# Two graph layers on one core: first tiles from contiguous copies, identity matmuls meanwhile, split products in another order, variances by Square, a ring of six tiles in layer 1, last y's steps moved by two tiles

## The reference

```
a1 = adj @ x;  a2 = adj @ x2                      # both times (2 + eps), then three dense layers each
h  = relu(h @ W[l].T + b[l])   for l in 0, 1, 2   # 128 x 128, one set of weights per branch
x  = layernorm(x + concat(h1, h2) @ Wm.T + bm)
A  = adj + I;  d = rsqrt(row sums of A)           # 0 where the sum is not positive
x  = layernorm(x + (d * (A @ (d * x))) @ W.T + b)
```

## Time and profile before

| | |
|---|---|
| median of 3 runs | 609.15 us (608.16 to 609.58) |
| the profiled execution | 609.65 us, its span 607.9 us |
| PE, matmuls | 589.8 us, 97% |
| DVE | 546.0 us, 90% |
| ACT | 368.5 us, 61% |
| DMA, mean | 233 GB/s |
| chain that ended last | PE 87%, DVE 9%, DMA, ACT and issue 1% each |

### The profile page before, as it was taken

One profiled execution on the slowest core, in us unless ns is written; L12 is line 12 of the kernel. 1 busy time (PEld: TensorE's weight loads), 2 busy tenths in 40 slices (PEclk: granted clock), 3 DMA queues, 4 the chain that ended last, 5 costly groups with the idle time before them and its releaser, 6 DMA issues.

```text
span 607.9 us, 7948 instructions
## 1 busy us (share of the span) xinstructions
PE 589.8 (97%) x2660; PEld 481.2 (79%) x2660; DVE 546.0 (90%) x697; ACT 368.5 (61%) x446; POOL 27.6 (5%) x31
## 2 busy tenths in 40 slices
PE   4999999999999999999999999999989999999996
PEld 3888888888888888888888888867758778778885
DVE  5999988997988997998799999966898988998997
ACT  6454337753454773363676355585867787787783
POOL 1000000001100000110000110000200010010011
PEclk9999999999999999999999999999999999999998
DMA  8968555433554533455543376584779999899921
GB/s 294 414 238 284 201 209 202 144 139 139 202 187 176 197 138 138 140 205 207 182 163 138 150 282 242 210 332 167 272 292 344 342 386 392 341 309 392 385 103 37
DMA packets 27833, 141.56 MB, mean 233 GB/s; under 512 B 2592, under 2 KB 3360, under 8 KB 13600
## 3 DMA queue, kind: packets, MB, share of 16 engines
q1 hardware_dynamic: 27376, 139.67, 62.2%
q10 hardware_dynamic: 432, 1.57, 0.6%
HBM read 139.14 MB, written 2.10 MB: 232 GB/s over the span
## 4 chain that ended last, share of the span: by engine, by line
PE 87%; DVE 9%; issue 1%; DMA 1%; ACT 1%; POOLq 0%; POOL 0%; SPq 0%; DVEq 0%; ACTq 0%
PE ps L409 75%; DVE alo L733 6%; PE pd L427 6%; PE ps L485 3%; PE pd L438 2%; PE pd L471 1%; DMA raw<-a_t 1%; DVE stats L805 1%; DVE z L906 1%; ACT ahi L582 1%; DVE mv L813 0%; DVE x1lo L872 0%; DVE xn L874 0%; DVE raw L888 0%; DVE raw L895 0%
## 5 line engine op out<-in xcount | busy, mean ns | idle before, releaser
L582 ACT ACTIVATE ahi<-raw 128x1024 fp32r<-128x1024 f32 x253 | 265.5, 1059 | 209.6 <-PE ps L409 196.6
L733 DVE TENSOR_TENSOR alo<-raw,ahi 128x1024 fp32r<-128x1024 f32 x253 | 304.7, 1217 | 46.6 <-ACT ahi L582 45.6
L409 PE MATMUL ps<-ahi,x2s 128*128 128x512 f32 x512 | 160.0, 391 | 0.0
L409 PE MATMUL ps<-ahi,x1hi 128*128 128x512 f32 x448 | 145.3, 400 | 12.0 <-DVE alo L726 8.0
L409 PE MATMUL ps<-alo,x1hi 128*128 128x512 f32 x448 | 141.2, 391 | 0.0
L409 PE MATMUL ps<-ahi,x1lo 128*128 128x512 f32 x448 | 141.0, 391 | 0.0
L409 PEld LDWEIGHTS ps<-ahi,x2s 128*128 128x128 f32 x512 | 96.7, 189 | 20.2
L409 PEld LDWEIGHTS ps<-ahi,x1hi 128*128 128x128 f32 x448 | 82.4, 189 | 37.3 <-issue 13.3
L409 PEld LDWEIGHTS ps<-alo,x1hi 128*128 128x128 f32 x448 | 84.6, 189 | 17.8
L409 PEld LDWEIGHTS ps<-ahi,x1lo 128*128 128x128 f32 x448 | 84.4, 188 | 17.8
L409 PE MATMUL ps<-alo,x2s 128*128 128x512 f32 x256 | 80.7, 391 | 0.0
(11 more groups left out here) (80 smaller groups left out, 348.7 us busy)
## 6 DMA issues: line engine op xcount, KB each, us to landing
raw<-a_t SPq DMA_DIRECT2D x108, 1024.0 KB, 4.8
raw<-a_t SPq DMA_DIRECT2D x39, 512.0 KB, 7.4
xn<-x SPq DMA_DIRECT2D x3, 1024.0 KB, 8.2
out<-outn ACTq DMA_DIRECT2D x3, 512.0 KB, 4.1
par<-params SPq DMA_DIRECT2D x1, 708.0 KB, 13.8
xn<-x SPq DMA_DIRECT2D x2, 256.0 KB, 4.8
raw<-a_t SPq DMA_DIRECT2D x2, 256.0 KB, 5.0
xn<-x SPq DMA_DIRECT2D x1, 512.0 KB, 7.9
```

The lines of the kernel that those rows point to most:

```text
L409: mm = pe.matmul(ps[bank][:, :], block_of(w, n), a[c], start=(n == 0 and k == 0), stop=(n == JB - 1 and k == 2))
L582: act.activation(ring_hi(n, last), raw_tile(layer, n), ACT.Copy).then_inc(hi_ready, 1)
L733: dve.tensor_tensor(ring_lo(n, last), raw_tile(layer, n), as_f32(ring_hi(n, last)), ALU.subtract).then_inc(lo_ready, 1)
```

## The change

- Start: three DRAM arrays take the place of strided reads: `head` (two halves of tile 0), `early` (tiles 1 to 7) and x12 in pieces. The first x piece is issued by ACT, not SP, so the halves of tile 0 are the first on SP. ACT rounds x's half of the piece, half a tile, x2's half, the other half.
- PE multiplies the identity by itself 8 times (128 x 128, float32) before tile 0; POOL makes the identity first.
- In every tile but those of the last quarter, PE takes the products with `ahi` first (hi by hi, hi by lo), then those with `alo`, and waits for `alo` only there.
- Layer 1: the ring has six places; the new ones are `hhi` and `alo_extra`. ACT and DVE steps beside layer 1 move by two tiles (`AHEAD_OF_PE`), among them `evacuate` from 2 to 4 and `copy_ay` from 1 to 3.
- The residual base of quarter 3 (two DVE instructions) moves from layer 1's tiles 7 and 8 to layer 0's tiles 20 and 21; the last y's bias from tile 24 to 30; its normalisation goes in blocks of four at tiles 20 and 21.
- Layer 1's variances: `accum_out` of residual2 gives the sum of z, ACT's Square with `accum_out` the sum of squares; bn_stats and bn_aggr go (but for the last quarter's tail).
- PE's loop over layer 1's quarters 1 and 2 is written out, since six does not divide 32.

```diff
-ACT_EVACUATE = 2
-ACT_RELU = tuple({k + SPLIT: l for k, l in plan.items()} for plan in PE_DENSE)
-DVE_RESIDUAL = tuple(k + SPLIT for k in PE_MERGE)
+PE_WARM = 8
+AHEAD_OF_PE = (SPLIT, SPLIT2)
+ACT_EVACUATE = (2, 4)
+ACT_RELU = tuple({k + ahead: l for k, l in plan.items()} for plan, ahead in zip(PE_DENSE, AHEAD_OF_PE))
+DVE_RESIDUAL = tuple(k + ahead for k, ahead in zip(PE_MERGE, AHEAD_OF_PE))
...
+        def slot(layer, q, n):
+            return (q * JB + n) % SPLIT2 if layer == 1 else n % SPLIT
...
+        def used_ahead(layer, q, n):
+            at = q * JB + (layer * QUARTERS * JB + n + 1)
+            if layer == 1 and q * JB + n >= SPLIT:
+                return at - SPLIT2 if q * JB + n >= SPLIT2 else 0
+            return at - SPLIT
...
-            load_x(0)
             for c in range(CH):
-                cols = slice(c * CW, (c + 1) * CW)
-                sp.dma_start(raw[:, 0, 0, cols], a_t[0][:, 0, cols]).then_inc(half_in[c], 16)
-            sp.dma_start(raw[:, 0, 1], a_t[0][:, 1]).then_inc(raw_in[0], 16)
+                sp.dma_start(raw[:, 0, 0, c * CW:(c + 1) * CW], head[c]).then_inc(half_in[c], 16)
+            sp.dma_start(raw[:, 0, 1], early[0]).then_inc(raw_in[0], 16)
...
+                    order = [(b, c, k) for b, c in banks for k in (0, 2, 1)]
+                else:
+                    order = [(b, c, k) for b in range(len(stationary)) for k in (0, 2) for c in range(CH)]
+                    order += [(b, c, 1) for b in range(len(stationary)) for c in range(CH)]
...
+                    if k == 1 and not lo_seen and not first:
+                        wait(pe, lo_ready, at)
+                        lo_seen = True
...
+            pe.wait_ge(warm_ready, 1)
+            for k in range(PE_WARM):
+                pe.matmul(pd[:, 3, 0:P], identity[:, :], identity[:, :], start=True, stop=True)
             layer0_quarter(0, None)
...
-                if n == ACT_EVACUATE:
+                if n == ACT_EVACUATE[plan]:
                     evacuate(q)
...
+            def square(q, blocks):
+                if blocks[0] == 0:
+                    wait(act, nmean_ready, q + 1)
+                    wait(act, out_written, q * 16)
+                for k in blocks:
+                    act.activation(outn[:, k * P:(k + 1) * P], z[:, k, :], ACT.Square, bias=nmean[:, k:k + 1],
+                                   accum_out=squares[:, k:k + 1]).then_inc(squares_ready, 1)
...
-            round_x(0)
+            _, k0, k1 = X_PIECES[0]
+            act.dma_start(xn[:, 0:2, k0 * P:k1 * P], x_piece(0)).then_inc(x_in[0], 16)
+            round_x(0, (0,))
...
-                                                 in1=xn[:, q, k * P:(k + 1) * P], op0=ALU.mult, op1=ALU.add)
+                                                 in1=xn[:, q, k * P:(k + 1) * P], op0=ALU.mult, op1=ALU.add,
+                                                 accum_out=zsum[:, k:k + 1])
```

More of the change, by code:

```diff
@@ L89, with build @@
 AHEAD = 3
-DVE_RESIDUAL2 = PE_PROJECT + SPLIT
+AHEAD2 = 5
+DVE_RESIDUAL2 = PE_PROJECT + SPLIT2
 DVE_STATISTICS2 = DVE_RESIDUAL2 + KB
-DVE_AGGREGATE2 = DVE_STATISTICS2 + KB // 2
-DVE_SHIFT2 = DVE_AGGREGATE2 + 3
-ACT_NORM2 = DVE_SHIFT2 + 2
+ACT_SQUARES = DVE_STATISTICS2 + 1
+DVE_VARIANCE2 = ACT_SQUARES + KB
+DVE_SHIFT2 = DVE_VARIANCE2 + 2
+ACT_NORM2 = DVE_SHIFT2 + 1
 X_PIECES = [(0, 0, 2), (0, 2, 4), (0, 4, KB), (1, 0, KB), (2, 0, KB), (3, 0, KB)]
 X_PIECE_AT = {KB * q + k: i for i, (q, k, _) in enumerate(X_PIECES)}
+X_PIECE_START = [2 * P * P * sum(k1 - k0 for _, k0, k1 in X_PIECES[:i]) for i in range(len(X_PIECES))]
 X_AFTER = {1: 1, 3: 2, 7: 3, 12: 4, 20: 5}
-def build(nc, a_t, x12, params, out):
+def build(nc, a_t, head, early, x12, params, out):
     with ExitStack() as ctx:
@@ L152, in build @@
         nshift = sb("nshift", [P, KB])
+        zsum = sb("zsum", [P, KB])
+        nmean = sb("nmean", [P, KB])
+        squares = sb("squares", [P, KB])
         degc = sb("degc", [P, KB])
@@ L536, in _ @@
             layer1_quarter(0, None)
-            with pe.Fori(1, QUARTERS - 1) as q:
+            for q in range(1, QUARTERS - 1):
                 layer1_quarter(q, q - 1)
@@ L577, in round_a @@
                             act.wait_ge(identity_added, identities(q, n))
-                last = layer == 1 and q == LAST
-                if not (last and n >= EXTRA):
-                    wait(act, block_used, q * JB + (layer * QUARTERS * JB + n + 1 - SPLIT))
-                act.activation(ring_hi(n, last), raw_tile(layer, n), ACT.Copy).then_inc(hi_ready, 1)
+                wait(act, block_used, used_ahead(layer, q, n))
+                act.activation(ring_hi(layer, q, n), raw_tile(layer, n), ACT.Copy).then_inc(hi_ready, 1)
             def round_h(q, l, m):
@@ L713, in _, with split_x @@
         def _(dve):
-            def split_x(i):
+            def split_x(i, pair=(0, 1)):
                 q, k0, k1 = X_PIECES[i]
-                for b in range(2):
+                for b in pair:
                     dve.wait_ge(x_hi, 2 * i + b + 1)
@@ L815, in aggregate, with variances @@
                         i.then_inc(stats_ready, 1)
-            def variances(done, r=slice(0, KB)):
-                wait(dve, stats_ready, done)
+            def variances(aggregated, r=slice(0, KB)):
+                wait(dve, stats_ready, aggregated)
                 dve.tensor_scalar(vareps[:, r], mv[:, r, 1], LN_EPS, None, ALU.add).then_inc(var_ready, 1)
@@ L944, in layer1_quarter @@
                         statistics_taken(QUARTERS * KB)
-                    elif before is not None and n == DVE_AGGREGATE2:
-                        statistics_taken((before + QUARTERS + 1) * KB)
                     split_a(q, 1, n)
```

164 lines of the change are left out of this document (99 added, 65 removed).

## The result

| | before | after |
|---|---|---|
| median of four runs each, same chip | 608.79 us (608.16 to 609.58) | 604.19 us (603.88 to 605.22) |
| the profiled execution | 609.65 us, span 607.9 | 603.97 us, span 602.1 |

What follows compares the result with a forecast made beforehand. PE was taken to bound the kernel. Start 3.0, turn -3.0, quarter 0 3.2, quarters 1 and 2 3.0, last quarter 0.3, tail -0.1 give 6.4 us: 602.8 us, own range 601.2 to 604.5, 8-in-10 range 600.3 to 605.9.

Steps and rivals of the forecast that it cites:

- The start: From program start to tile 8: first product at 6.3 us, tile 8 at 29.8; 3.0 us gained, ends 1.0 and 3.7.
- The turn: Layer 0 to layer 1: PE waits for ACT's copy of ps0 behind two roundings; 3.0 us lost (2.8 to 3.2).
- The rival that the clock falls there: Clock falls in PE's pause between layers 0 and 1: price up to 3.0, taken 2.4, total 605.2 us; chance 0.15.
- Quarter 0 of layer 1: From tile 8 to quarter 1: waits for alo go, a y wait stays; 3.2 us gained, ends 2.0 and 5.2.
- The waits for alo: Layer 1, quarter 0: PE's waits for DVE's alo go, with ACT and DVE two tiles further and ahi products first.
- The wait for y: Layer 1, tile 24: PE still waits 2.0 us for the last y's remainder x1lo.
- Quarters 1 and 2: Layer 1: DVE loses 8 bn_stats (2.2 us) per quarter and has more lead; 3.0 us gained, ends 0 and 3.3.
- ACT becomes the bound: Quarters 1 to 3: a Square costs 0.8 instead of 0.4 us, PE waits about 1 us per quarter; 605.8 us, chance 0.12.
- The last quarter and the tail: Last quarter's alo wait gives 0.3 us, the tail's accumulations cost 0.1; together +0.2 us.
- The moved residual base: Layer 0's last quarter: 2 x 1.14 us more on DVE, covered by 2.4 us of slack; without cover up to 2.3 us.
- The sum: All terms together: 6.4 us gained against the profiled execution, 603.25 us; median of the runs 0.5 lower, 602.8 us.

## Why the prediction was right, and where not

- **The start** was mis-sized: 4.1 us, not 3.0. The landing of the half tile was put between 4.4 and 5.7 us; it was there at 3.46, and x's piece, at 4.40, became the last operand, so PE started at 5.51 and not 6.3. The rows had 4.41 for that piece's use, the end I did not take. Read with strides the half lands at 4.82 and x's piece at 6.03, and the first product starts at 7.13: so the layout is worth 1.6 us there, and the prediction had no number of its own for it. The clock was up at the first product, not near 10; this bought less than it seems, since DVE then sets tile 8's start, as the prediction said (it put DVE's remainder at 29.1, it ended at 28.6). The rule of the Trainium skill (DMA: Bandwidth & Descriptors, section "Issuing engines are not separate DMA queues") would have made the term smaller. Here the issue of the second half moved by 0.9 us and its landing by 2.0, so more than issue time was at stake; why, these runs don't show.
- **The turn** was right in place, cause and size: 3.01 us, and 2.7 in the profile (3.6 of medians, with the clock's part) when its cause was taken away. The rival that the clock falls there had 0.15. It did not happen in the profiled execution, but in six of the eight profiled executions here that have this pause (not in that of the changed kernel and of the one with the old order), at 1.4 to 1.6 us. The Trainium skill (TensorE: Matmul & The Clock Gate, section "HAM oscillation — how this bites in real kernels") says that the products after a pause start cold; in its example the pauses are about 3 to 5 us. These traces agree in six of eight, and the rival's chance was too small.
- **Quarter 0 of layer 1** is the step that failed: 3.2 forecast, 1.0 came. The waits for alo went as forecast: from tile 8 to tile 24's wait PE takes 21.7 us instead of 24.1. The wait for y was 2.3 and not 2.0, small; behind it the clock fell, for 1.6, a term that the prediction weighed at the turn only. "The 1.6 us wait at 446.5 didn't lower it" was the argument against, and it was about a shorter wait: in every profile with the 2.3 us pause (six) the clock fell, with 1.75 us (the kernel before, and the one with the old order of products) it did not. A slip in the reading is without weight: tile 8's first product starts at 420.44, and the 420.68 of the earlier trace rows is where the record ahead of it ends, so 5.6 us were lost there and not 5.3.
- **Quarters 1 and 2** had the right sum, 3.2 for 3.0, for a reason that is half wrong. Part of the reasoning was DVE's load without bn_stats; with bn_stats back, nothing is lost. What came with the ring and the order of the products was enough; the ring's own share is not shown. A Square costs ACT 0.38 to 0.40 us with its read, 0.40 forecast; the row of the accumulator's read stands below. So the rival "ACT becomes the bound" did not occur. Where the pause for y was removed, ACT did use up its lead and PE waited 1.7 us at one turn, but by ACT's wait for nmean and not by the price of a Square, which was this rival's condition.
- **The last quarter and the tail** gave 0.6 for 0.2; this was not followed further. The moved residual base cost nothing to speak of: layer 0 from tile 8 to its last product takes 362.58 us, 0.13 more than before.
- **The sum** is 5.8 by spans (6.4 forecast); the errors of +1.1 at the start and -2.2 in quarter 0 partly cancel; that the sum came out nearer than these two terms is luck. The median is 1.4 us above the forecast: half is the sum, half that the median was taken 0.5 us below the profiled execution, as before, and came out 0.2 above it.

## What to carry to other kernels

When a ring gets deeper and steps are renumbered with it, look at each instruction that was written between the old and new number: a rounding that waits for the last product must not stand ahead of the copy that lets the next product start. A pause of the bounding engine is also the time in which the others catch up, so removing it can uncover their next lateness; read their lead over the bounding engine tile by tile before and after. And a gain is not shown to come from the part that was meant to bring it until that part has been taken out alone.

## What the runs showed of the hardware

ACT's Squares with an accumulator, timeline of the changed kernel, quarter 1:

```profile
477.23 0.39 ACT L696 ACTIVATE outn<-z,nmean 128x128 f32<-128x128 f32 x1
477.52 0.19 ACT L696 ACTIVATION_READ_ACCUMULATOR outn<-z,nmean 128x1 f32 x1
477.61 1.05 ACT L623 ACTIVATE ahi<-raw 128x1024 fp32r<-128x1024 f32 x1
```

- The read of the accumulator has a record of 0.19 us, but the next instruction starts 0.09 after the read's start: they overlap, and Square and read take 0.38 together (477.23 to 477.61). DVE's read has a record of 0.08.
- The same pause did not always lower the clock: 3.0 us at the turn in six of eight profiles, 2.3 us at y in six of six, 1.75 in neither of two (the kernel before and the one with the old order). A fall there cost 1.4 to 1.6 us. In other executions of the kernel with the copies ahead a mean clock of 0.999 says that it stayed up behind y too.
- At the program's start the view shows a granted clock of 1.00 while products stand 0.43 us apart (in the kernel without identity products, and in the one with bn_stats). There the level is to be read from the pace: the 16 identity records take 3.39 to 3.79 us at the start and 1.95 us in the middle of the program.
